# Attention for a post-norm transformer layer: one written-out schedule, a second pass 12 heads behind, and stacks moved inside SBUF

## The reference

```
x: 16 batches x 256 tokens x 128, 16 heads of 8
q = x @ Wq + bq
latent = x @ Wl + bl                      # 32 wide
k = latent @ Wk + bk;  v = latent @ Wv + bv
attn = softmax(q k^T * 8**-0.5)           # per batch and head, 256 x 256
x = layernorm(x + (attn @ v) @ Wo + bo)
S = sigmoid(x @ Wg).T;  G, I = top_k(S, 1024)          # per expert, over all 4096 tokens
out = (gelu(x[I] @ W1 + b1) @ W2 + b2) * G             # per expert
x = layernorm(x + scatter_add(out at I))
```

## Time and profile before

| | |
|---|---|
| median of 3 runs | 707.22 us (706.48 to 711.65) |
| span of the profiled execution | 716.2 us, first to last instruction |
| PE, DVE, ACT, POOL busy | 65%, 49%, 41%, 32% of the span |
| first first pass starts | 44.5 us |
| last logits of attention | 421.3 us |

### The profile page before, as it was taken

One profiled execution on the slowest core, in us unless ns is written; L12 is line 12 of the kernel. 1 busy time (PEld: TensorE's weight loads), 2 busy tenths in 40 slices (PEclk: granted clock), 3 DMA queues, 4 the chain that ended last, 5 costly groups with the idle time before them and its releaser, 6 DMA issues. The chain is left out here.

```text
span 716.2 us, 11487 instructions
## 1 busy us (share of the span) xinstructions
PE 463.8 (65%) x3477; PEld 354.1 (49%) x3477; DVE 352.1 (49%) x1039; ACT 294.2 (41%) x549; POOL 230.6 (32%) x249
## 2 busy tenths in 40 slices
PE   2248594895968959869499830174888687759000
PEld 1035373663756647557377520143777476648000
DVE  5046374673854738637468348793233323322006
ACT  1106274572754736627456654050433223213005
POOL 7701011020020200201100000155588778777750
PEclk9659798897986979969779955555899878979555
DMA  6143313213122131221310005302144344333354
GB/s 175 65 127 104 109 42 114 63 44 115 50 88 82 33 120 56 68 90 42 109 52 19 2 1 164 93 16 48 36 70 71 76 74 69 49 56 33 30 94 166
DMA packets 53559, 52.21 MB, mean 73 GB/s; under 512 B 5299, under 2 KB 43158, under 8 KB 53526
## 3 DMA queue, kind: packets, MB, share of 16 engines
q1 hardware_dynamic: 41222, 41.04, 18.4%
q0 software_dynamic: 11264, 8.66, 9.3%
q10 hardware_dynamic: 1040, 2.10, 1.0%
HBM read 28.32 MB, written 23.20 MB: 72 GB/s over the span
## 5 line engine op out<-in xcount | busy, mean ns | idle before, releaser
L701 ACT ACTIVATE probs<-banks 128x512 f32<-128x512 f32 x256 | 147.9, 599 | 144.2 <-PE banks L905 141.8
L1092 DVE TENSOR_REDUCE row_max<-banks 128x2 f32<-128x512 f32 x256 | 170.0, 681 | 70.9 <-PE banks L859 69.0
L905 PE MATMUL banks<-q_stack,k_second 128*128 128x256 f32 x512 | 112.7, 305 | 66.2 <-DMA q_stack<-shift_t 63.3
L859 PE MATMUL banks<-k_first,q_stack 128*128 128x256 f32 x512 | 130.2, 342 | 0.7 <-DVE row_max L1092 0.7
L905 PEld LDWEIGHTS banks<-q_stack,k_second 128*128 128x128 f32 x512 | 85.8, 207 | 71.4 <-issue 45.9
L615 POOL DMA_INDIRECT summed<-v_ones,to_index x64 | 100.4, 1568 | 28.7 <-issue 20.5
L859 PEld LDWEIGHTS banks<-k_first,q_stack 128*128 128x128 f32 x512 | 86.4, 210 | 26.5 <-DVE row_max L1092 15.4
L755 ACT ACTIVATE hT<-banks,b_cols 128x512 f32<-128x512 f32 x64 | 42.3, 687 | 110.7 <-PE banks L1027 89.0
L1042 PE MATMUL banks<-w_buf,hT 128*128 128x128 f32 x512 | 69.2, 294 | 10.6 <-ACT hT L755 9.2
L1042 PEld LDWEIGHTS banks<-w_buf,hT 128*128 128x128 f32 x512 | 67.1, 209 | 14.2 <-issue 6.1
L601 POOL DMA_INDIRECT taken<-x_table,from_index x64 | 64.3, 1005 | 29.0 <-issue 23.9
(11 more groups left out here) (197 smaller groups left out, 671.0 us busy)
## 6 DMA issues: line engine op xcount, KB each, us to landing
k_first<-k_split SPq DMA_DIRECT2D x64, 96.0 KB
q_stack<-q_split SPq DMA_DIRECT2D x64, 96.0 KB
k_split<-k_hi SPq DMA_DIRECT2D x16, 256.0 KB
q_split<-q_hi SPq DMA_DIRECT2D x16, 256.0 KB
w_buf<-in_L_ffn_W SPq DMA_DIRECT2D x16, 256.0 KB
x_table<-rows SPq DMA_DIRECT2D x1, 2176.0 KB, 15.5
x_pair<-in_L_attn_x SPq DMA_DIRECT2D x8, 256.0 KB, 5.9
k_split<-k_lo SPq DMA_DIRECT2D x8, 256.0 KB
```

What stands on the lines that cost most here:

```text
L701: s.activation(probs[:, 4 * (r % 2) + gg], ps_second[:, k % 2], ACT.Exp, scale=SCALE).then_inc(exp_done, 1)
L859: mm = t_.matmul(o, q_stack[:, side, r, gg, i * P:(i + 1) * P], k_first[:, side, gg], start=True, stop=True)
L905: mm = t_.matmul(ps_second[:, k % 2, j * SEQ:(j + 1) * SEQ], k_second[:, h.side, gg, j * P:(j + 1) * P], q_stack[:, h.side, r, gg], start= ...
L1092: v.tensor_reduce(row_max[:, r, 2 * gg:2 * gg + 2], ps_first[:, FIRST_BANK[k]].rearrange("p (i j) -> p i j", i=2), AX, ALU.max).then_inc(f ...
```

## The change

The change replaces the whole attention stretch and its start; routing and the experts keep their instructions and get other buffers (among them `xc_all`, which is now laid over `hT`, and the centred rows, which stay in `rows`).

- **Stacks.** The copies in DRAM go. The parts move from SBUF to SBUF: three DMAs of 256 KB a pair for the queries (`stack_q`) and twelve of 64 KB for the keys (`stack_k`), each of the latter onto 8 partitions. Queries of four heads share a stack, and the keys of each lane are padded with zeros for the other heads' rows (`k_pad`). The maxima are four rows, with a row of -1 in the keys for each lane (`signs`). The copy `k_second` made by ACT (line 672) goes.
- **Schedule.** There is no loop. Each engine runs through 285 steps; step s does the first pass of head s and the second pass of head s - 12. Jobs stand at fixed steps of a batch or a pair, and "max" stands at step 4t + 5 of the batch, for heads 4t to 4t + 3. ACT copies the maxima out, and POOL makes both the high and the low part.
- **K and V from x.** `Wl` is multiplied with `Wk` and `Wv` once at the start (`wlkv`), so the latent job goes, and q, k and v come straight from `xT`.
- **Start.** The first pair's parts are made a batch at a time, with ACT issuing eight of the key DMAs, the memsets are cut into pieces of 512 columns and shared with DVE, and ACT reorders `Wq`.

```diff
-MAX_AT = {1: "max3", 8: "max0", 11: "max1", 13: "max2"}
...
+LAG = 12
...
+PREP_STEP = {"xT": 3, "q": 7, "k": 11, "v": 15}
+TAIL_STEP = {"norm": 32, "oT": 34, "y": 36, "xcT": 42, "logits": 44}
...
+            at.setdefault(16 * b + 4 * t + 5, []).append(("max", 4 * b + t))
...
-            def store_split(pair, uses_of):
-                for job, cut, stored, hi, lo_, dram, hi_terms in (
-                        ("k", k_cut, k_stored, k_hi, k_lo, k_split, (0, 2)),
-                        ("q", q_cut, q_stored, q_hi, q_lo, q_split, (0, 1))):
-                    copied_out(sp, job, uses_of)
-                    for t in hi_terms:
-                        sp.dma_start(dram[pair, :, t].rearrange("r d g s i -> r (d g s i)"),
-                                     hi[:].bitcast(F32)).then_inc(stored, 16)
-                    sp.wait_ge(cut, pair + 1)
-                    sp.dma_start(dram[pair, :, 3 - sum(hi_terms)].rearrange("r d g s i -> r (d g s i)"),
-                                 lo_[:].bitcast(F32)).then_inc(stored, 16)
-            def load_k(pair, side):
-                for r in range(NR):
-                    sp.dma_start(k_first[32 * r + DH:32 * r + 32, side].rearrange("p g i -> p (g i)").bitcast(F32),
-                                 k_split[pair, r, :, :, :, side].rearrange("t d g i -> (t d) g i")
-                                 ).then_inc(k_first_in[side], 16)
...
-            def half(h):
-                if h.prep:
-                    store_split(h.n + 1, h.uses)
-                load_shift("max3", h.uses, h.side)
-                if h.ahead:
-                    if h.prep:
-                        sp.wait_ge(k_stored, STORES * (h.n + 2))
-                    sp.wait_ge(first_full, 16 * (h.b + 1))
-                    sp.wait_ge(k_kept, h.b + 1)
...
-                    sp.wait_ge(q_stored, STORES * (h.n + 2))
-                for r in range(NR):
-                    if h.ahead:
-                        sp.wait_ge(second_full, 16 * h.b + 4 * r + 4)
-                        load_q(h.n + 1, h.side, r)
-                    if r < 3 and h.nxt:
-                        load_shift(f"max{r}", h.uses, h.after)
...
+            def first_half(side, q_sem, k_sems):
...
+                sp.wait_ge(first_q_hi, side + 1)
+                for term in (0, 1):
+                    sp.dma_start(q_stack[q_rows(term), 0, :, cols].bitcast(F32), q_hi[:, cols].bitcast(F32)
+                                 ).then_inc(q_sem, 16)
+                sp.wait_ge(first_q_cut, side + 1)
+                sp.dma_start(q_stack[q_rows(2), 0, :, cols].bitcast(F32), q_lo[:, cols].bitcast(F32)).then_inc(q_sem, 16)
+                sp.wait_ge(first_k_hi, side + 1)
+                sp.wait_ge(keys_zeroed[0], 4)
+                for c in range(LANES):
+                    lane = slice(32 * c, 32 * c + 32)
+                    if c == 0:
+                        sp.wait_ge(first_k_cut, side + 1)
+                    sp.dma_start(k_pad[k_rows(1, c), 0, c, :, cols].bitcast(F32), k_lo[lane, cols].bitcast(F32)
+                                 ).then_inc(k_sems[c], 16)
+                        for term in (0, 2):
+                            sp.dma_start(k_pad[k_rows(term, c), 0, c, :, cols].bitcast(F32),
+                                         k_hi[lane, cols].bitcast(F32)).then_inc(k_sems[c], 16)
+            first_half(0, first_q_in, first_k_in)
+            sp.wait_ge(signs_made, 1)
+            def load_signs(i):
+                for c in range(LANES):
+                    sp.dma_start(k_pad[ROWS_1:ROWS_2, i, c].bitcast(F32).rearrange("p t (s j) -> p (t s) j", s=2),
+                                 signs[ROWS_1:ROWS_2, c].unsqueeze(1).to_broadcast([LANES, 2 * T_GROUPS, SEQ])
+                                 ).then_inc(signs_in[i], 16)
+            load_signs(0)
+            first_half(1, after_in, [after_in] * LANES)
+            def load_shift(b, t):
+                copied_out(sp, ("max", 4 * b + t))
+                sp.dma_start(q_stack[ROWS_1:ROWS_2, b // 2 % 2, t, b % 2 * SEQ:(b % 2 + 1) * SEQ].bitcast(F32),
+                             shift_t[:, t].bitcast(F32)).then_inc(shift_in[t], 16)
+            def stack_q(pair):
+                if pair > 1:
+                    sp.wait_ge(second_full, 32 * (pair - 1))
+                sp.wait_ge(q_cut, pair)
+                for term, kind in enumerate(Q_TERMS):
+                    sp.dma_start(q_stack[q_rows(term), pair % 2].bitcast(F32),
+                                 (q_hi if kind == "hi" else q_lo)[:].bitcast(F32)).then_inc(stack_in[pair % 2], 16)
+            def stack_k(pair, lanes):
+                if pair == 1:
+                    sp.wait_ge(keys_zeroed[1], 4)
+                sp.wait_ge(k_cut, pair)
+                for c in lanes:
+                    for term, kind in enumerate(K_TERMS):
+                        sp.dma_start(k_pad[k_rows(term, c), pair % 2, c].bitcast(F32),
+                                     (k_hi if kind == "hi" else k_lo)[32 * c:32 * c + 32].bitcast(F32)
+                                     ).then_inc(stack_in[pair % 2], 16)
...
+            for b in range(BATCHES):
+                pair, side = divmod(b, 2)
+                for t in range(T_GROUPS):
+                    load_shift(b, t)
+                    if side == 0 and t == 0 and pair + 2 < PAIRS:
+                        load_x(pair + 2)
+                    if side == 0 and pair + 1 < PAIRS:
+                        if t == 2:
+                            stack_q(pair + 1)
+                        elif t == 3:
+                            stack_k(pair + 1, (0, 1))
+                    if side == 1 and pair + 1 < PAIRS and t == 0:
+                        stack_k(pair + 1, (2, 3))
+                    if b == 1 and t == 1:
+                        load_signs(1)
...
+            for c in (2, 3):
+                for t in range(T_GROUPS):
+                    ins = g.memset(k_pad[:, 0, c, t].bitcast(F32), 0.0)
+                ins.then_inc(keys_zeroed[0], 1)
+            for c in range(LANES):
+                for t in range(T_GROUPS):
+                    ins = g.memset(k_pad[:, 1, c, t].bitcast(F32), 0.0)
+                ins.then_inc(keys_zeroed[1], 1)
+            for i in range(2):
+                for side in range(2):
+                    for j in range(2):
+                        ins = g.memset(v_ones[:, i, side, j], 0.0)
...
+            def split(pair, job, full, hi, lo_, rounded, cut):
+                copied_out(pool, (job, pair))
+                if pair > 1:
+                    pool.wait_ge(stack_in[(pair - 1) % 2], stacked_before(pair - 1))
+                else:
+                    pool.wait_ge(after_in, 16 * STACKED)
+                passed(pool, pool_waits)
+                g.tensor_copy(hi[:], full).then_inc(rounded, 1)
+                pool.wait_ge(rounded, pair)
+                g.tensor_tensor(lo_[:], full, hi[:].bitcast(F32), ALU.subtract).then_inc(cut, 1)
...
+            act.wait_ge(first_k_hi, 1)
+            act.wait_ge(keys_zeroed[0], 4)
+            for c in range(LANES):
+                for term in (0, 2):
+                    act.dma_start(k_pad[k_rows(term, c), 0, c, :, 0:SEQ].bitcast(F32),
+                                  k_hi[32 * c:32 * c + 32, 0:SEQ].bitcast(F32)).then_inc(first_k_in[c], 16)
+            first_hi(1, "q", first_q, q_hi, ps_second[:, 0], bq_col, first_q_hi)
+            first_hi(1, "k", first_k, k_hi, ps_second[:, 1], bk_col, first_k_hi)
...
+                if c == 0:
+                    pe.wait_ge(shift_in[t], 16 * (b + 1))
...
+                if h > 1:
+                    pe.wait_ge(exp_done, h - 1)
...
+                    mm = t_.matmul(ps_second[:, h % 2, j * SEQ:(j + 1) * SEQ], k_pad[0:ROWS_2, n % 2, c, t, at:at + P],
...
+            for step in range(LAST_STEP + 1):
+                for job in JOBS_AT.get(step, ()):
+                    run_job(job)
+                if step < STEPS:
+                    first_pass(step)
+                if 0 <= step - LAG < STEPS:
+                    second_pass(step - LAG)
+                if step >= PV_STEP and (step - PV_STEP) % 4 == 0 and (step - PV_STEP) // 4 < 4 * BATCHES:
+                    pv((step - PV_STEP) // 4)
...
+                    mm = t_.matmul(bank, wq[:] if kind == "q" else wlkv[:, 0], xT[:], start=True, stop=True)
...
+                        mm = t_.matmul(bank[:, c * P:(c + 1) * P], xT[:, c * P:(c + 1) * P], wlkv[:, 1], start=True,
+                                       stop=True)
...
+            for c in (0, 1):
+                for t in range(T_GROUPS):
+                    ins = v.memset(k_pad[:, 0, c, t].bitcast(F32), 0.0)
+                ins.then_inc(keys_zeroed[0], 1)
```

More of the change, by code:

```diff
@@ new lines, in schedule, with numbers @@
+def schedule():
+    at = {}
+    for b in range(BATCHES):
+        for t in range(T_GROUPS):
+            at.setdefault(16 * b + 4 * t + 5, []).append(("max", 4 * b + t))
+        for job, step in TAIL_STEP.items():
```

(49 more changed lines are left out.)

924 lines of the change are left out of this document (412 added, 512 removed).

## The result

The changed kernel takes 630.68 us in the median of four runs (627.64 to 634.22); the kernel before, run beside it, 707.41 (706.48 to 711.65). The ratio is 0.891, with a 95% interval of 0.886 to 0.897. The forecast was 610, with a range of 594 to 648. The profiled execution took 629.71 us, of which 628.0 are its span.

A forecast was written before the change was run, and what follows sets the result against it. PE was taken as the bound once its 63.3 us of shift waits go: 43 (start) + 4 (slow clock) + 256 (steps) + 21 (end) = 324, plus 294.9 = 619 span, less 9 = 610 us, range 594 to 648.

The forecast's parts named there:

- the shift's place behind the stores: Attention before: 4 KB DMA of turned maxima queued behind 1.5 MB of stores, 63.3 us in seven PE waits, to go.
- the step: Steady attention: PE sets the pace, 16.8 us a batch or 1.05 us a step; 244 steps take 256 us.
- the end: From the last first pass to the logits: second pass trails by 12 heads, 21 us.
- that last burst: Last six key DMAs of a pair land by 32 us for a need at 33.6; lateness taken as 0.
- the key stacks are slow: Rival, chance 0.17: few DMA engines serve 8 partitions, each pair's keys 3 us late, 21 us in all, 632 us.
- The two rules: Key stacks: engine rule gives them 8 DMA engines; SBUF port page gives 1.2 us per 64 KB key DMA.
- The start: Up to the first second pass: reached near 36 us, waits for the first shift to about 43.
- The early start: Rival, chance 0.12: DVE gets the port at the first gap between POOL's memsets, 11 us less, 599 us.
- The tight chain: Rival, chance 0.14: PE waits for DVE at the turning of the maxima, 18 us more, 628 us.
- Stalls kept: Rival, chance 0.04: the pairs' stalls simply remain, 8 us a pair kept, 666 us.
- slower than before: Rival, chance 0.03: shift caught behind stacks draining at 33 GB/s or less; 855 us on one engine.
- The 9 us taken off the span: Whole kernel: span before 716.2 against median 707.2, so 9 taken off the forecast span of 619 us.

The follow-up runs named there:

- experiment 8: Kernel before, SP's queue reordered so the shift of group 3 goes ahead of a pair's stores and group 0's between key and query stores: 703.26 us, ratio 0.993.
- experiment 1: Changed kernel without stacking the third key term of pairs 1 to 7, eight key DMAs a pair instead of twelve: 607.07 us, ratio 0.857.
- experiments 1 and 6: Changed kernel, third key term of pairs 1 to 7 not stacked (1: 607.07 us) or copied by POOL instead of DMA (6: 609.05; with POOL's memset wait 597.58).
- Experiment 5: Changed kernel with one wait added on POOL, which zeroes the second key buffer only after the weights are reordered: 614.83 us, ratio 0.869.
- experiment 4: Changed kernel with DVE taking each maximum over the first 128 of 256 columns only: 622.17 us, ratio 0.880.
- experiment 7: On the 597.58 us kernel (POOL key copies, gap in POOL's memsets): first shifts earlier 599.57; turning a step later 598.55; both 604.59; centred rows' turning later 596.43 us.

## Why the prediction was right or wrong

**The direction held, and the stalls went as forecast.** The seven waits of 8 to 11 us are gone. The cause that the prediction gave them, the shift's place behind the stores, was not the whole of it (experiment 8, and the last paragraph here). Without the transfers the step was sized well: 1.05 us forecast, 1.037 in experiment 1. In the changed kernel itself it is 1.126, and by the prediction's own sign ("wrong if the step is not 1.05 us") the forecast of the steps failed. Well sized were the end (21 and 21.5), the copy of `wkv` (end at 16 forecast, 16.6 measured) and POOL and ACT without queues of waits. The last maximum was forecast for 303 and came at 321.1, the logits for 324 and came at 342.1.

**The step that failed: "what is next late is that last burst, with 1 to 2 us in hand. I take 0 for it."** The issues were followed rightly and the bytes were not. The same holds for the shift between the two groups of keys: it was to land 27 us into the pair for a need at 30, and it is there 31.6 us in (247.09 - 215.47), 1 us late. The drain was taken between 17 us and a quarter of it, from the rate of the stores; but a DMA from SBUF to SBUF moves 7.4 to 8.9 GB/s on each engine where the stores moved 21.9, and the key stacks use half of the engines. So 0.79 MB of queries take 6 us and 0.79 MB of keys 12, which is about the upper bound, and in the pair shown they start at 231.6, 16 us into it, and move until some 35. The term that was put at 0 cost 273.7 - 252.0 = 21.7 us: 11.4 of waiting and 10.3 of slow clock. The forecast of the steps was 8 too high without it (260 for 252), which leaves the 13.7.

**The rival "the key stacks are slow" is what happened.** Its condition was half right: not two of sixteen engines serve 8 partitions but about half of them (share 0.56), and each moves a third of what it moved in the stores; experiments 1 and 6 show the cost by taking four key DMAs away. That its 632 came so near was luck, since its terms were off both ways: 1.4 us for 64 KB were forecast and 1.0 measured, 3 us a pair of waiting forecast and 11.6/7 = 1.7 measured, and the slow clock, for which it said only that it "may cost some", made up for it. Its place was only half of it. It named line 873; the larger part is at line 893, for a shift behind the first six keys. The prediction said that none of those would be left in the pairs.

**The two rules.** The share of 0.56 while keys move agrees with the Trainium skill ("DMA: Bandwidth & Descriptors", on why a DMA increments its semaphore by 16), by which the key stacks get 8 engines. The estimate worked out from the ports (the Trainium skill, "SBUF — State Buffer", the DMA port swizzle), 1.2 us for a key DMA, came near the measured 1.0, but the runs give no sign of the cause it names: the queries, spread over 32 partitions, run at nearly the same rate per engine as the keys over 8. Why both run at about a third of the stores' rate per engine was not tried.

**The start** was 3.9 late at the first second pass. The high part of the keys was ready at 23.9 (22.5), and ACT's eight issues took 0.96 each, not 0.8, so the second batch's list began near 32 and the first shift went out at 45.1 (41). **The early start** did not happen: DVE stayed out until POOL's chain ended: 32 memsets back to back, and DVE got in at none of their joints. The Trainium skill ("SBUF — State Buffer", on who interferes with whom) has the one who starts first hold the pair for one instruction; here it was held for the chain. Experiment 5 shows that a real gap, one wait, is enough. The rival's 11 us were the right price of that wait at the first second pass (11.4).

**The tight chain** exists and is small: 3 to 9 us (experiment 4) for the 18 forecast, and moving the turning by a step gains nothing (experiment 7). **Stalls kept and slower than before** did not happen. The second decided at 33 GB/s; the keys move at 66.

**The 9 us taken off the span** were right in size, and most of them now have a place. The stretch from the logits on took 294.9 and 285.9. In the profiled execution of before, the matmuls of line 1007 start at 490.81, pause several times with nothing that they wait for in the profile, and DVE reads their result at 499.15, 8.3 us later; in that of the changed kernel the same takes 1.1 (411.68 to 412.76). ACT, behind them, sits 13.5 and 6.2 us ahead of a table load. In the run of experiment 8, where that part is the kernel before's, the stretch took 704.7 - 418.8 = 285.9 as well. So it is a thing of that one execution, not of the change; why PE paused there was not found.

**What the change owes its gain to** is not the shift's place in the queue, which the first part of the prediction named. Experiment 8 takes that away and leaves 703. What is left as the cause of the stalls' end is that the queries and keys no longer have to be stored and loaded before they can be used; no run keeps the rest of the change and brings the round trip back. How much of the 76.7 us is due to the other parts (twelve heads behind and not sixteen, K and V without the latent step, the start) was not tried apart.

## What to carry to other kernels

Price a transfer by direction and by engines: find a row of the same direction, divide its rate by its share of 16 engines, and see how many engines it will use (here a slowest dimension of 4 went with a share of 0.26, 8 with 0.56, 32 with 1.05); then follow the bytes through the schedule, not the issues. A burst as long as its room makes everything behind it late, the 4 KB that is urgent too. Here neither an earlier place nor another queue helped, only fewer bytes: look for copies that an idle engine can make on chip. And before blaming the transfer that a wait names, ask what would be waited for if it were in time.

## What the runs showed of the hardware

A DMA from SBUF to SBUF moved 7.4 GB/s per DMA engine to 8 partitions (66 GB/s at a share of 0.56, 238 to 250) and 7.6 to 8.9 to 32 (127 at 1.05, 107 at 0.75), in 2 KB pieces; the loads of `x` in the same kernel moved 120 GB/s with 0.40 of the engines, 19 each. This is the window of such a load:

```profile
222.00:224.00 2.00, 2.00 (x15) 1.52 (x12) 1.21 (x4) 0.96 (x2) 0.00 (x0) 1.00 0.40 120
```

DVE's work from SBUF to SBUF waits for POOL in the steady state too. Once a pair, in the changed kernel, POOL's subtraction and DVE's centring meet:

```profile
225.21 1.28 POOL L525 TENSOR_TENSOR q_lo<-kq_full,q_hi 128x512 fp32r<-128x512 f32 x1
225.21 1.55 DVE L1173 TENSOR_SCALAR rows<-resid,mv_all 128x128 f32<-128x128 f32 x2
...
226.91 0.41 PE L845 MATMUL banks<-ident,rows 128*128 128x128 f32 x2 [0.45 <-DVE rows L1173]
```

Two centrings alone take 2 x 0.28; here they take 1.55, which is POOL's 1.28 and one of them. DVE's maxima, which read PSUM, go on beside POOL at their 0.69 (the one at 224.63, beside POOL's cast at 224.51, took 0.66).
